# Later places for the small transfers, the totals and the power of a two-layer convolution kernel's averages

## The reference

```
# layer 0: a long 2D convolution whose filter is an outer product, hx along rows, hy along columns
y   = irfft2(rfft2(x) * rfft2(hx outer hy))[:256, :256];  x1 = y + x * bias[channel]
# layer 1: scores of each row with all rows, weighted and summed, then a norm over the channel
red  = sum_t( (x1 @ x1^T)[s, t] / 16 * weights[channel][s, t] )      # one number a row
y2   = x1 + red
out  = (y2 - mean) * rsqrt(var + 1e-5) * gamma + beta                # mean, var over 4x256x256 of a channel
```

## Time and profile before

| | us |
|---|---|
| median of 3 runs (lowest to highest) | 1038.53 (1032.49 to 1047.23) |
| the profiled execution | 1034.5 |
| its span in the trace | 1032.5 |
| mean granted TensorE clock | 0.978 |

### The profile page before, as it was taken

How to read it: one execution, slowest core, us unless ns; L and a number is a source line. 1 busy time by engine, 2 the same in 40 slices (tenths; PEclk the granted TensorE clock), 3 DMA queues, 4 the chain that set the end, 5 groups by cost and what they waited for, 6 DMA issues and landing times.

```text
span 1032.5 us, 18894 instructions
## 1 busy us (share of the span) xinstructions
PE 957.4 (93%) x5308; PEld 822.5 (80%) x5308; DVE 762.8 (74%) x2460; ACT 672.7 (65%) x1088; POOL 669.1 (65%) x518
## 2 busy tenths in 40 slices
PE   8999899999999899989989989999989899999993
PEld 6888778888788788878878877878878778788882
DVE  2687668787688677868767767777776877788885
ACT  2447467677577576767656666766756766676765
POOL 2776566776676665767666757666747668577750
PEclk9999999999999999999989999999999999999996
DMA  7677868876878888877777987868769768788944
GB/s 228 224 202 180 264 192 277 270 222 245 270 219 251 249 224 257 272 213 255 258 196 258 216 249 265 242 232 269 235 225 268 211 239 255 229 277 270 254 132 168
DMA packets 91439, 244.23 MB, mean 237 GB/s; under 512 B 17312, under 2 KB 42272, under 8 KB 83232
## 3 DMA queue, kind: packets, MB, share of 16 engines
q1 hardware_dynamic: 73280, 235.73, 72.9%
q10 hardware_dynamic: 18144, 8.33, 4.5%
HBM read 176.65 MB, written 67.37 MB: 236 GB/s over the span
## 4 chain that ended last, share of the span: by engine, by line
issue 42%; POOL 35%; PE 16%; DVE 2%; DMA 2%; ACT 1%; POOLq 1%; ACTq 0%; DVEq 0%
POOL xl L387 12%; POOL zl L402 7%; PE ps_c L507 6%; POOL toep L380 6%; POOL wl L395 6%; PE ps_u L507 6%; PE ps_z L507 4%; POOL rstd L364 3%; POOL stat L357 1%; DMA everyone<-partition_moments 1%; DMA toep_whole<-filters_padded 0%; ACT zh L491 0%; DVE products L702 0%; ACT out_sb L482 0%; POOLq L133 0%
## 5 line engine op out<-in xcount | busy, mean ns | idle before, releaser
L402 POOL TENSOR_TENSOR zl<-z_sb,zh 128x1024 fp32r<-128x1024 f32 x126 | 302.3, 2399 | 316.1 <-ACT zh L491 314.3
L507 PE MATMUL ps_u<-toep,xh 128*128 128x256 f32 x1016 | 242.1, 320 | 38.4 <-DVE ul L733 35.9
L482 ACT ACTIVATE out_sb<-z_sb,shift,gain 128x256 f32<-128x256 f32 x496 | 257.7, 593 | 29.2 <-DMA partition_moments<-own 21.4
L507 PE MATMUL ps_z<-uh,toep 128*128 128x512 f32 x768 | 273.5, 410 | 0.1
L702 DVE CUSTOM_DVE_ANT_0 products<-z_sb,ps_c 128x256 bf16<-128x256 f32 x508 | 183.5, 418 | 93.5 <-PE ps_c L507 93.4
L507 PE MATMUL ps_c<-zh,wh 128*128 128x512 f32 x508 | 200.4, 394 | 18.0 <-POOL zl L402 17.0
L507 PEld LDWEIGHTS ps_u<-toep,xh 128*128 128x128 f32 x1016 | 165.7, 196 | 55.7 <-issue 45.1
L733 DVE TENSOR_TENSOR ul<-ps_u,uh 128x1024 fp32r<-128x1024 f32 x127 | 151.7, 1195 | 71.1 <-ACT uh L448 71.1
L507 PE MATMUL ps_u<-toep_whole,xt_sb 128*128 128x128 f32 x1016 | 200.4, 279 | 0.0
L507 PE MATMUL ps_c<-zh,wl 128*128 128x512 f32 x508 | 198.0, 390 | 0.0
L507 PE MATMUL ps_c<-zl,wh 128*128 128x512 f32 x508 | 197.9, 390 | 0.0
(11 more groups left out here) (72 smaller groups left out, 985.1 us busy)
## 6 DMA issues: line engine op xcount, KB each, us to landing
xt_sb<-xt_in SPq DMA_DIRECT2D x64, 1024.0 KB, 10.0
x_sb<-x_in SPq DMA_DIRECT2D x128, 512.0 KB, 8.6
out<-out_sb SPq DMA_DIRECT2D x124, 512.0 KB, 6.1
w_sb<-wt_in SPq DMA_DIRECT2D x64, 256.0 KB, 7.0
toep_whole<-filters_padded SPq DMA_DIRECT2D x64, 256.0 KB, 6.7
everyone<-partition_moments ACTq DMA_DIRECT2D x63, 128.0 KB, 7.8
out<-z_sb SPq DMA_DIRECT2D x4, 512.0 KB, 3.0
partition_moments<-own ACTq DMA_DIRECT2D x63, 1.0 KB, 4.4
```

The source lines that it names most:

```text
L402: nc.gpsimd.tensor_tensor(zl[:, zs.slot(2)], z_sb[:, r, h], zh[:, zs.slot(2)].bitcast(F32), ALU.subtract)\
L482: last = nc.scalar.activation(to[:, k, b], z_sb[:, r, h, k, b], ACT.Identity, bias=shift[:, r, g:g + 1], scale=gain[:, r])
L507: return nc.tensor.matmul(o, a, b, start=start, stop=stop)
```

## The change

ACT issues both small transfers behind the norm of its stage, ahead of `zh`, and no longer ahead of the norm. DVE does `totals` at the end of the even stage of lag 8, behind `statistics`, and no longer at its start. POOL does the power in the odd stage of lag 9 behind `toep` and `xl` (`wl` falls in even stages), ahead of `zl`, and no longer first. Lags, buffers and instructions are the same; PE's and SP's orders are unchanged.

```
--- before.py
+++ after.py
@@ -365,10 +365,6 @@
 
             def stage(st):
 
-                vs = st.trail(LAG_POWER)
-                if starts(vs) and not ending(vs, 4):
-                    inverse_deviation(vs)
-
                 ms = st.trail(LAG_MEAN)
                 if starts(ms):
                     shift_means(ms)
@@ -394,6 +390,10 @@
                     wait_chan(pool, wh_ready, ws, 1)
                     nc.gpsimd.tensor_tensor(wl[:, r], w_sb[:, r], wh[:, r].bitcast(F32),
                                             ALU.subtract).then_inc(wl_ready, 1)
+
+                vs = st.trail(LAG_POWER)
+                if starts(vs) and not ending(vs, 4):
+                    inverse_deviation(vs)
 
                 zs = st.trail(LAG_Z)
                 if active(zs) and not ending(zs, 2):
@@ -447,19 +447,6 @@
                     wait(act, y_done, us, -1)
                     nc.scalar.activation(uh[:, us.slot(2)], u_bank(us)[:, :, :, :], ACT.Copy)\
                         .then_inc(uh_ready, 1)
-
-                ms = st.trail(LAG_MEAN)
-                if starts(ms) and not ending(ms, 2):
-                    r = ms.ring(XR)
-                    wait_chan(act, mean_in, ms, 1)
-                    nc.scalar.dma_start(own_dram[r:r + 1, :].rearrange("o (p n) -> (o p) n", n=2), own[:, r])\
-                        .then_inc(gathered, 16)
-                ss = st.trail(LAG_SPREAD)
-                if starts(ss) and not ending(ss, 2):
-                    act.wait_ge(gathered, ss.channel(1) * 16)
-                    nc.scalar.dma_start(everyone[:, ss.ring(2), 0:2 * P],
-                                        bass.AP(own_dram, ss.ring(XR) * 2 * P, [[0, P], [1, 2 * P]]))\
-                        .then_inc(spread[ss.ring(2)], 16)
 
                 no = st.trail(LAG_NORM)
                 if starts(no) and not ending(no, 2):
@@ -482,6 +469,19 @@
                             last = nc.scalar.activation(to[:, k, b], z_sb[:, r, h, k, b], ACT.Identity,
                                                         bias=shift[:, r, g:g + 1], scale=gain[:, r])
                     last.then_inc(norm_done, 1)
+
+                ms = st.trail(LAG_MEAN)
+                if starts(ms) and not ending(ms, 2):
+                    r = ms.ring(XR)
+                    wait_chan(act, mean_in, ms, 1)
+                    nc.scalar.dma_start(own_dram[r:r + 1, :].rearrange("o (p n) -> (o p) n", n=2), own[:, r])\
+                        .then_inc(gathered, 16)
+                ss = st.trail(LAG_SPREAD)
+                if starts(ss) and not ending(ss, 2):
+                    act.wait_ge(gathered, ss.channel(1) * 16)
+                    nc.scalar.dma_start(everyone[:, ss.ring(2), 0:2 * P],
+                                        bass.AP(own_dram, ss.ring(XR) * 2 * P, [[0, P], [1, 2 * P]]))\
+                        .then_inc(spread[ss.ring(2)], 16)
 
                 zs = st.trail(LAG_Z)
                 if active(zs):
@@ -715,10 +715,6 @@
                 last.then_inc(bn_ready, 1)
 
             def stage(st):
-                vs = st.trail(LAG_TOTAL)
-                if starts(vs):
-                    totals(vs)
-
                 gs = st.trail(LAG_NORM)
                 if starts(gs):
                     gain_and_offset(gs)
@@ -741,6 +737,10 @@
                     reduce_rows(cs, ps_c)
                 if active(zs) and not ending(zs, 2):
                     statistics(zs)
+
+                vs = st.trail(LAG_TOTAL)
+                if starts(vs):
+                    totals(vs)
 
             run_steps(dve, PAIRS, 2 * UNROLL, END_STEPS, stage)
```

## The result

| | before | after |
|---|---|---|
| median, us (lowest to highest) | 1038.61 (1032.49 to 1047.23), 4 runs | 957.86 (957.47 to 960.78), 4 runs |
| profiled execution / its span, us | 1034.5 / 1032.5 | 957.5 / 955.0 |
| mean granted TensorE clock | 0.978 | 0.990 |

The ratio is 0.9223, with a 95% interval of 0.9155 to 0.9291. The forecast was 959, its sum for the profiled execution 957.1.

What follows compares the result with a forecast made beforehand. PE, busy 93% of the span, was taken as the limit. Profiled execution 1034.5 - 78.4 (time off PE's floor) + 1.0 (tail) = 957.1 us; with half of the 4.0 us scatter, forecast 959, range 951 to 987.

Steps and rivals of the forecast that it cites:

- 78.4 us: Between pairs 3 and 127: PE's time beyond its floor of 7.114 us a pair, all taken as won.
- The tail's term of +1.0: At the end: the last everyone is issued behind a norm, costing 0 to 2.1 us, taken as 1.0.
- Rival D: DVE's waits are not the cause, so moving them changes nothing: 1035 us; chance 0.08, shared with part of Rival A.
- The 25.5 us beside the idle time: On PE: lost time beyond 52.9 us of idle time, read as slow matmuls at 1.2 GHz behind stalls.
- the predicted 1.5 us earlier: ACT's even stage: the norm starts 1.5 us earlier, near 908.3 for 909.81, covering all waits for zl.
- on the edge: POOL's odd stage: the power, if left first, would find veps ready only about when it starts, 929.4 against 929.5.
- the 8.5 us: ACT ahead of zh: own, issued at 910.4 at the latest, may take 8.5 us to land before PE loses time.
- half of the 4.0 us: Profiled execution was 4.0 us below the runs' median; half was kept as scatter, giving 959.
- Rival A: ACT ahead of zh: own lands late in every channel, up to 1097 us; 0.08 shared with Rival D to 1055, 0.05 beyond.
- Rival C: Memory traffic becomes the limit: 985 us if the mean stays at 260 GB/s; chance 0.17, shared with another rival.
- 10.0 us: In Rival A: own's landing estimated as its longest, 8.2 us, plus 1.8 for HBM at high load; about 1049 us.

Runs made afterwards that it cites:

- e1_totals_only: The kernel before with only DVE's totals moved to the end of the even stage; 960.92 us, ratio 0.9239.
- e7_no_wait: The kernel before with totals still first but reading the transfer of the channel before, so only the wait goes (wrong averages, timing only); 966.42 us, ratio 0.9309.
- e4_power_first: The changed kernel with POOL's power back at the head of its stage; 957.23 us, ratio 0.9211.
- e9_norm_ends: The changed kernel with ACT waiting for the end of the norm's fourth ACTIVATE before issuing own; 964.2 us, ratio 0.9325.
- e5_hop2: The changed kernel with the 1 KB of own sent twice, one after the other, before everyone is issued; 1320.0 us, ratio 1.2761.
- e3_power_only: The kernel before with only POOL's power moved behind toep and xl; 1035.83 us, ratio 0.9973.

## Why the prediction was right

**The sum.** The large term, 78.4 us off the floor of 7.114 us a pair, was right to 0.2 us. The span changed by -77.5: the start took 1.65 us more (pair 3 at 38.18 for 36.53), the tail 0.7 less (34.76 us from pair 127 to the end, for 35.44). The tail's term of +1.0 had the wrong sign. The start varies between executions (36.4 to 38.3 in these traces, and both ends occur in kernels with the same order up to there) and has no link to the change. So the start's +1.65, at nothing in the sum, and the tail's -0.7, at +1.0, nearly cancel out: that the sum of 957.1 meets the profiled 957.5 so closely is in part luck.

**The cause.** DVE's wait for `everyone` in front of `ul` was the loss. e1_totals_only shows it from one side (the move alone brings 78 us), e7_no_wait from the other (the wait alone, taken away in place, brings 70). Rival D is out.

**The 25.5 us beside the idle time.** They went too, but the prediction's reading of them, matmuls at the low clock behind a stall, covers only a part. Between pair 3 and pair 127, before and after (us, busy by engine, PEclk, DMA share, GB/s):

```profile
36.53:997.11 960.58, 907.74 (x5085) 783.74 (x5084) 727.55 (x2346) 639.66 (x1031) 648.82 (x493) 0.98 0.79 239
...
38.18:920.24 882.06, 882.06 (x5086) 776.55 (x5085) 715.83 (x2340) 650.22 (x1032) 647.79 (x493) 1.00 0.88 261
```

PE was busy 25.7 us longer before, for the same matmuls. The clock records of the trace grant 1.2 GHz in seven stretches there, 30.7 us together; each lies in, or within 1.5 us behind, a stall in which PE waited 2.1 to 4.8 us for `ul`. After the change there is none. At half speed 30.7 us cost at most 15.4. The other 10 us lie at a granted clock of 1.00: a pair with a stall shows 0.16 us more busy time at the median where PE waited for `ul`, 0.33 where it waited for `zl`. What these are is not shown; ends of matmuls are modelled in this profile.

**ACT.** The norm came the predicted 1.5 us earlier. But its worth was overrated by the attention it got: with `totals` moved, both transfers' new places bring 3.7 us (e1_totals_only against e4_power_first), alone they bring nothing.

**POOL.** Nothing, as predicted; also "on the edge" was right in kind: put back first, the power waits in every channel and nobody notices.

**The step that was wrong: the 8.5 us.** The prediction had `own` issued at the end of the norm, 2.7 us behind the start of DVE's `own`, and so a room of 8.5 us against a longest landing of 8.2. The issue comes 0.7 to 0.8 us behind DVE's `own`. The end of the room was read well: 10.3 us from there, some 0.2 earlier than the prediction had it, and 0.15 of these are the time from `zl`'s end to PE's start, which it left out. And 8.2 was not the longest: landings reached 9.4 in the change and 9.9 in e4_power_first. With the predicted issue the kernel loses about 7 us, as e9_norm_ends shows. The conclusion "nothing is lost" was right, but for the wrong reason: two errors, an issue 1.9 us too late and a longest landing 1.2 us too short, cancel out. The margin, 0.3 us in the prediction, was 0.9 us in the profiled execution and 0.3 in that of e4_power_first.

**The scatter.** The forecast kept half of the 4.0 us between profiled execution and median, as scatter of the stalls. Of that 0.4 was left (957.47 against 957.86), so the forecast is 1.1 us too high.

**Rival A** has the right mechanism and the right price per us (e5_hop2: slope one), and did not come, since 1 KB issued ahead of or with SP's group landed within 10.2 us in every run (the longest in e1_totals_only). **Rival C**: a fifth of the DMA share was said to be left; the change took half of that, 0.81 to 0.90, and no engine waits for `xt_sb` or `x_sb`; ACT's waits for a store sum to 6.1 us, and PE does not feel them. The 0.2 to 2 us that the Trainium skill's "DMA: Bandwidth & Descriptors" gives for an access to HBM in "Latency and other measured facts", used in the prediction to make 10.0 us out of 8.2, point the way of the trace for `everyone` (1.0 us later at the median, at denser traffic). The longest landings of `own`, 9.4 in the change and 9.9 in e4_power_first, come near that 10.0, but no run separates that access from the rest of the landing. The same page's turn-taking between queues, packet by packet ("Queues, rings and completion order"), which would spare the small transfer, agrees with e9_norm_ends (4.8 us at the start of the group) and does not explain the 9.4 us of e5_hop2's second hop; what makes the difference within the group stays open.

## What to carry to other kernels

Find the floor first: the pace of the bound engine over some repetitions without a wait, times their number, says what any reordering can win, here to 0.2 us between pairs 3 and 127. Then look for the one wait on a transfer that stands ahead of the work the bound engine needs, and move the consumer, not the transfer, to the last place at which its result is still in time. A place in program order is not a time for a transfer's issue: read in the trace when it goes out, and how much room its longest landing has, before trusting that it is free. One execution does not show the longest landing: for `own` it was 8.2 us in the trace of before and 9.3 in e3_power_only.

## What the hardware showed that was not expected

- An issue of a transfer behind four ACTIVATEs of 0.6 us each went out 0.2 us after the first of them began (191.80 against 191.62), with `own` already done; in 61 of 63 channels it went out while the norm ran. Only a wait on the last one's own semaphore held it back (e9_norm_ends, 295.12).
- 1 KB to DRAM took 2.5 to 11.7 us (both in e5_hop2). Issued with SP's group of about 2.5 MB it took 4.8 us at the median (e9_norm_ends), issued some 5 us into the group 9.4 us (e5_hop2). Two executions of the same kernel had medians of 5.7 and 4.6.
- PE's pace repeats to 0.01 us: at the floor each pair took 7.11 or 7.12 us, at a mean of 268 GB/s of traffic (100 to 900 us) as at 172 (900 to 914 us).
- A stall of PE costs more than its length: 52.8 us of idle time between pairs 3 and 127 came with 25.7 us more busy time, at most 15.4 of them by the granted clock.
